# Gated cross-attention and expert layer on one core: the attention's output projection as three fp32r products of high and low parts, and the second norm applied by ScalarE

## The chip, the core and the metric

One core of a Trainium2 chip runs the whole program. The metric is the device time of one execution in microseconds (us), median of several runs. The granted TensorE clock over the profiled execution was 0.991 of full speed. The engines are named as in the profile: PE is TensorE (PEld its weight loads), DVE is VectorE, ACT is ScalarE, POOL is GpSimd, SP is SyncE, which here only starts transfers.

## The reference

```python
def xattn(query, key_value, Wq, bq, Wk, bk, Wv, bv, Wo, bo):   # 16 heads of 16
    q = (query @ Wq + bq).reshape(B, Nq, H, D).transpose(0, 2, 1, 3)
    k = (key_value @ Wk + bk).reshape(B, Nkv, H, D).transpose(0, 2, 1, 3)
    v = (key_value @ Wv + bv).reshape(B, Nkv, H, D).transpose(0, 2, 1, 3)
    attn = softmax(clip(einsum('bhqd,bhkd->bhqk', q, k) * D ** -0.5, -1e4, 1e4))
    x = einsum('bhqk,bhkd->bqhd', attn, v).reshape(B, Nq, Cq)
    return x @ Wo + bo
x = x + tanh(g_xattn[0]) * xattn(layernorm(x), ctx_768, ...)      # x: (8, 512, 256), ctx_768: (8, 512, 192)
x = x + tanh(g_ffn[0]) * ffn(layernorm(x), ...)                   # 8 experts of 1024, dense, gated by their logits
```

Everything is float32. The layer norm has no weights: `(x - mean) / sqrt(var + 1e-5)` over the 256 columns.

## The kernel before, in words

The program has three stages. The first (`build_project`, up to about 92 us) computes queries, keys and values of the 8 batch entries, as products of fp32r high and low parts, and stores them to DRAM. The second (`attend_programs`, about 92 to 537 us) is the attention, its output projection, the residual, the second layer norm and the expert logits. The third computes the eight experts (`expert_programs`), and its first tiles begin among the last steps of the second.

The change lies in the second stage. It runs a pass for each batch entry b, and the order in a pass is written out by hand. A pass has 4 groups g of 4 heads, each group 4 blocks k (the four 128-row tiles of keys), each block 4 places. A slot is written (g, k, place), a block (g, k). In a slot PE does one `scores_T` product (`ps_t`, L862: transposed scores of one head, 49 rows by 512 columns) and one `scores` product for the group two ahead (`ps_s`, L851, 48 rows). The two lie in different row halves of the array and start together, and I call them a pair. ACT takes `ps_t` with an exponential (L1170, into `probs_T` or `w_raw`), DVE takes `ps_s` with a row minimum (`low`, L1007). Each side has three banks, so that the pair of a slot waits for the exponential and the minimum of three slots before. At place 3 PE also does `probs_v` of the block before (`ps_o`, L873, 8 records).

Between these stand units, each of which fills the one bank `ps_m`, which has to be emptied before the next unit. The table `SHARED` says behind which pair PE does a unit, `VECTOR_AT` and `SCALAR_AT` at which slots DVE and ACT do their part of it. The entries are (kind, 0 for this batch entry or -1 for the one before, number). The kinds are:

- `low` (L879): the minima of a group turned, taken by ACT (L1181) and sent by SP into `q_st`;
- `out` (L884): the heads of a group turned, after ACT has copied `ps_o` into `o_sb` (`copy`, L1175); DVE divides by the sums (`normalise`, L1025 to L1030) into `attn`;
- `rows` (L890): `attn` of the entry before turned in two halves, taken by ACT as `attn_T` (L1186);
- `y` (L898, `project_out`): `attn_T` times `Wo`, in two halves of two token tiles. A tile is 2 fp32 products of 128 by 128 by 256 columns. The first half is done in two pieces, at (0, 3, 2) and (1, 0, 0) (`HALVES`). DVE adds it to the residual (`add_residual`, L1040);
- `x2T` (L905): the residual turned, taken by ACT; `xnT` (L911): the normed rows turned, taken by ACT as `x_hi` (L1198) and by DVE as `x_lo` (`split`, L1091);
- `logits` (L919, 4 fp32r products of 512 columns) and, once in four entries, `pick` (L926).

Without a bank, DVE does `statistics` (L1048) and `norm` (L1082: subtract the mean, multiply by the reciprocal root), `check` (L1013, L1015), and POOL computes the reciprocal root between those two (L803 to L827). The units with -1 belong to the entry before, so pass 0 has none of them, and after pass 7 a closing sequence does those of the last entry among the first tiles of the experts.

```python
    for k in range(TT):
        ...
        for place in range(GROUP):
            scores_T(b, g, k, place, turn)
            if exists(ahead[0]):
                scores(*ahead, place, turn + ahead[0] - b)
            if place == V_PLACE and exists(back[0]):
                probs_v(*back)
            first_half(b, HALVES.get((g, k, place)))
            shared(b, SHARED.get((g, k, place)))
```

## Time and profile before

| | |
|---|---|
| median of 3 runs | 1896.85 us (1896.41 to 1897.63) |
| the profiled execution, its own time | 1896.23 us |
| its span, first to last instruction | 1894.4 us |
| PE, DVE, ACT, POOL busy over the span | 98%, 68%, 67%, 8% |
| starts of the eight passes (first `ps_t`) | 112.4, 161.3, 212.0, 262.7, 313.4, 365.1, 415.8, 466.5 us |

The profile has one execution. Busy time of PE is that of its matmul records, whose ends are modelled, so a full PE row doesn't say that nothing waits: starts of neighbouring records say more. [...]

### The profile page before, as it was taken

The numbers are of one execution on the slowest core, as the hardware profiler recorded it, in microseconds if no ns is written. First come the engines' busy times: TensorE is split into PE (matmuls) and PEld (weight loads), VectorE is DVE, ScalarE is ACT, GpSimd is POOL, SyncE is SP. The second block draws the span as 40 slices with busy tenths as digits, with TensorE's granted clock in tenths as the row PEclk, the third lists the DMA queues.
The fourth block names the chain that finished last, engine by engine and source line by source line (L and its number), as shares of the span: only waits on it lengthen the run. The fifth ranks groups of instructions, "written<-read, shape, count | busy, mean of one in ns | idle before, by whom it ended". The sixth has DMA issues, their size and how long they took to land.

```text
span 1894.4 us, 25738 instructions
## 1 busy us (share of the span) xinstructions
PE 1862.6 (98%) x8868; PEld 1349.0 (71%) x8868; DVE 1291.1 (68%) x2279; ACT 1277.7 (67%) x2145; POOL 146.9 (8%) x327
## 2 busy tenths in 40 slices
...
GB/s 284 374 81 84 87 91 88 79 88 110 38 50 129 107 210 151 119 117 110 90 111 89 133 138 124 95 112 112 89 112 129 151 93 117 111 90 89 121 101 58
DMA packets 97245, 220.84 MB, mean 117 GB/s; under 512 B 31314, under 2 KB 49492, under 8 KB 87892
## 3 DMA queue, kind: packets, MB, share of 16 engines
...
q14 instruction: 64, 0.52, 0.1%
...
## 4 chain that ended last, share of the span: by engine, by line
PE 89%; ACT 3%; DVE 2%; issue 1%; POOL 0%; ACTq 0%; DVEq 0%; POOLq 0%
PE ps_y L2169 32%; PE ps_h L2116 28%; PE ps_t L862 7%; PE ps_o L873 6%; PE ps_h L2089 5%; PE ps_y L2101 4%; PE ps_s L851 2%; PE ps_m L898 2%; PE ps_m L884 1%; ACT w_raw L1170 1%; DVE low L1007 1%; PE ps_m L890 0%; ACT gelu L2366 0%; PE ps_m L919 0%; PE ps_m L905 0%
## 5 line engine op out<-in xcount | busy, mean ns | idle before, releaser
L2469 DVE TENSOR_TENSOR h_lo<-gelu,h_hi 128x512 fp32r<-128x512 f32 x512 | 352.8, 693 | 437.0 <-ACT h_hi L2369 405.7
L2116 PE MATMUL ps_h<-x_hi,w_pair 128*128 128x512 f32 x1568 | 562.3, 392 | 1.8 <-ACT gelu L2366 0.8
L2366 ACT ACTIVATE gelu<-early,b 128x512 f32<-128x512 f32 x336 | 243.2, 724 | 229.5 <-DVE early L2618 220.7
L2116 PEld LDWEIGHTS ps_h<-x_hi,w_pair 128*128 128x128 f32 x1568 | 294.3, 188 | 78.3 <-issue 6.0
L1007 DVE TENSOR_REDUCE low<-ps_s 128x1 f32<-128x512 f32 x512 | 322.1, 681 | 26.1 <-PE ps_s L851 23.1
L2369 ACT ACTIVATE h_hi<-gelu 128x512 fp32r<-128x512 f32 x448 | 283.5, 633 | 41.9 <-ACT gelu L2366 1.1
L2116 PE MATMUL ps_h<-x_lo,w_pair 128*128 128x512 f32 x784 | 309.4, 395 | 0.0
L2618 DVE TENSOR_TENSOR early<-ps_h,copy 128x512 f32<-128x512 f32 x336 | 230.5, 686 | 49.4 <-PE ps_h L2116 49.4
L1170 ACT ACTIVATE probs_T<-ps_t 128x512 f32<-128x512 f32 x384 | 206.4, 594 | 45.5 <-PE ps_t L862 44.6
L851 PE MATMUL ps_s<-k_st,q_st 48*128 48x512 f32 x512 | 205.0, 481 | 3.2 <-SPq L755 2.0
L2169 PE MATMUL ps_y<-h_hi,w_lo 128*128 128x512 f32 x512 | 202.7, 396 | 0.0
L2169 PE MATMUL ps_y<-h_hi,w_hi 128*128 128x512 f32 x512 | 202.4, 395 | 0.0
L2169 PE MATMUL ps_y<-h_lo,w_hi 128*128 128x512 f32 x512 | 202.0, 394 | 0.0
L862 PE MATMUL ps_t<-q_st,k_st 49*128 49x512 f32 x512 | 190.4, 456 | 3.6 <-ACT probs_T L1170 2.7
L862 PEld LDWEIGHTS ps_t<-q_st,k_st 49*128 49x128 f32 x512 | 84.0, 188 | 131.8 <-ACT probs_T L1170 54.3
L2116 PEld LDWEIGHTS ps_h<-x_lo,w_pair 128*128 128x128 f32 x784 | 147.2, 188 | 32.7
L2169 PE MATMUL ps_y<-h_hi,w_first_lo 128*128 128x512 f32 x384 | 152.0, 396 | 0.0
L2169 PE MATMUL ps_y<-h_hi,w_first_hi 128*128 128x512 f32 x384 | 151.8, 395 | 0.0
L2169 PE MATMUL ps_y<-h_lo,w_first_hi 128*128 128x512 f32 x384 | 151.6, 395 | 0.0
L2169 PEld LDWEIGHTS ps_y<-h_hi,w_lo 128*128 128x128 f32 x512 | 96.2, 188 | 23.2
L2169 PEld LDWEIGHTS ps_y<-h_hi,w_hi 128*128 128x128 f32 x512 | 96.0, 188 | 22.8
L2169 PEld LDWEIGHTS ps_y<-h_lo,w_hi 128*128 128x128 f32 x512 | 96.1, 188 | 22.3
...
## 6 DMA issues: line engine op xcount, KB each, us to landing
...
x_lo<-blocks_scratch SPq DMA_DIRECT2D x28, 768.0 KB, 10.2
...
q_st<-q_scratch SPq DMA_DIRECT2D x192, 64.0 KB, 2.3
k_st<-k_scratch SPq DMA_DIRECT2D x192, 64.0 KB, 2.3
...
```

Of the source, the lines that this page charges most:

```text
L851: pe.matmul(ps_s[bank_of(turn, at)][:], q_st[g][rows, j // 2, t * P:(t + 1) * P], k_st[g][rows, j // 2, :], start=True, stop=True).then_in ...
L862: pe.matmul(ps_t[bank_of(turn, at)][:], k_st[g][rows, j // 2, k * P:(k + 1) * P], q_st[g][rows, j // 2, :], start=True, stop=True).then_in ...
L873: mm = pe.matmul(ps_o[32 * j:32 * j + VW, :], v_st[g][:, k, j, :], probs_T[k][:, j, :], start=(k == 0), stop=(k == TT - 1))
L1007: dve.tensor_reduce(low[:, g % 2, column:column + 1], ps_s[bank_of(turn, at)][:], AX_X, ALU.min).then_inc(low_done, 1)
L1170: act.activation(probs_T[k][:, turned_head(b, g, k, i), :], ps_t[bank_of(turn, (g * TT + k) * GROUP + i)][:], ACT.Exp, scale=-1.0).then_in ...
L2089: mm = pe.matmul(ps_h[:, j % RING, :], w[:, k, at], x[:, k, bass.ds(c * SEQ, SEQ)], start=(i == 0), stop=(i == len(parts) - 1))
L2116: mm = pe.matmul(bank, w[wp], x[xp], start=start and n == 0, stop=n == 2, skip_group_check=not start)
L2169: mm = pe.matmul(ps_y[s][:, d, :], w[:, j, at], h[:, c, :], start=(i == 0 and c < 2 and m == 0), stop=(i == QUADS - 1 and c >= 2 and m == 2))
L2366: act.activation(gelu[:, c % GELUS, :], src, ACT.Gelu_apprx_tanh, bias=b1[p][:, j:j + 1]).then_inc(gelu_done, 1)
L2369: act.activation(h_hi[:, c, :], gelu[:, c % GELUS, :], ACT.Copy).then_inc(h_hi_done, 1)
L2469: dve.tensor_tensor(h_lo[:, j % RING, :], gelu[:, j % GELUS, :], h_hi[:, j % RING, :].bitcast(F32), ALU.subtract).then_inc(h_ready, 1)
L2618: dve.tensor_tensor(corner[c // 2], bank, copies[0 if c == 3 else 1][:], ALU.add).then_inc(corner_done, 1)
```

## The change

- `Wo` is loaded in the second stage (into the space of `attn`) and no longer in the first. ACT copies it to `wo_hi` and POOL subtracts it to `wo_lo`, both fp32r, once, before the first pass. PE and DVE wait for that.
- ACT's part of `rows` now writes `attn_hi` (fp32r), and DVE has a part of its own, `rows_low`, which writes `attn_lo` and frees the bank. `attn_lo` lies in the space of `xn`, so it also waits until `xn` of the entry before is turned.
- `project_out` does 6 fp32r products of 256 columns for a tile where there were 2 fp32 products: high by high, high by low, low by high, for both halves of the contraction.
- `norm` moves from DVE to ACT as `Identity` with scale (reciprocal root) and bias. POOL computes that bias, minus mean times root, with one more instruction. In the closing sequence DVE still does it.
- All three tables are written anew, `HALVES` excepted.
- `logits_T` holds one set of four entries and no longer two.

Per pass, the units of PE that stand at another slot are `out` of the entry before (0,1,2) to (0,1,1); `rows` 0 (0,2,2) to (0,1,2) and `rows` 1 (0,2,3) to (0,2,1); `low` 2 (1,1,3) to (1,0,3); `y` 1 (1,1,1) to (1,1,2); `out` 0 (1,2,0) to (1,2,2); `x2T` (1,3,0) and (2,0,2) to (1,3,1) and (2,0,1); `low` 3 (2,1,0) to (2,1,2); `out` 1 (2,2,1) to (2,2,0); `xnT` (2,3,1) and (3,0,0) to (2,3,2) and (3,0,2); `low` 0 of the next entry (3,1,3) to (3,1,0); `out` 2 (3,2,1) to (3,1,2); `logits` (3,3,0) to (3,2,1); `pick` (3,3,3) to (3,3,0).

```diff
 SHARED = {
-    (0, 0, 2): ("low", 0, 1), (0, 1, 2): ("out", -1, 3), (0, 2, 2): ("rows", -1, 0), (0, 2, 3): ("rows", -1, 1),
+    (0, 0, 2): ("low", 0, 1), (0, 1, 1): ("out", -1, 3), (0, 1, 2): ("rows", -1, 0), (0, 2, 1): ("rows", -1, 1),
...
 VECTOR_AT = {
+    (0, 1, 0): [("check", 0, 1), ("out", -1, 3)], (0, 1, 3): [("rows", -1, 0)], (0, 2, 3): [("rows", -1, 1)],
...
 SCALAR_AT = {
+    (0, 0, 1): [("low", 0, 1)], (0, 0, 2): [("copy", -1, 3)], (0, 1, 1): [("rows", -1, 0)], (0, 2, 2): [("rows", -1, 1)],
...
+    (2, 0, 3): [("copy", 0, 1)], (2, 1, 2): [("low", 0, 3), ("norm", -1, 0)], (2, 1, 3): [("norm", -1, 1)],
+    (2, 2, 0): [("norm", -1, 2)], (2, 2, 3): [("norm", -1, 3)], (2, 3, 1): [("xnT", -1, 0)], (3, 0, 1): [("xnT", -1, 1)],
...
@@ sync
+        sp.dma_start(wo_raw, io["Wo"].rearrange("(k p) n -> p k n", p=P)).then_inc(wo_loaded, 16)
@@ gpsimd
+        pool.wait_ge(wo_hi_done, 1)
+        pool.tensor_tensor(wo_lo[:], wo_raw, wo_hi[:].bitcast(F32), ALU.subtract).then_inc(wo_split, 1)
...
-            pool.tensor_tensor(rstd, root, dev, ALU.add).then_inc(rstd_done, 1)
+            pool.tensor_tensor(rstd, root, dev, ALU.add).then_inc(moment_done, 1)
+            pool.wait_ge(moment_done, first + 10)
+            pool.tensor_tensor(shift, mean, rstd, ALU.mult).then_inc(rstd_done, 1)
@@ tensor
+            parts = [(a, w, k) for k in range(KT) for a, w in ((attn_hi, wo_hi), (attn_hi, wo_lo), (attn_lo, wo_hi))]
             for t in tiles:
                 t0 = (2 * i + t) * P
-                for k in range(KT):
-                    mm = pe.matmul(ps_m[:, t * DIM:(t + 1) * DIM], attn_T[:, k, t0:t0 + P], wo[:, k, :],
-                                   start=(k == 0), stop=(k == KT - 1))
+                for n, (a, w, k) in enumerate(parts):
+                    mm = pe.matmul(ps_m[:, t * DIM:(t + 1) * DIM], a[:, k, t0:t0 + P], w[:, k, :],
+                                   start=(n == 0), stop=(n == len(parts) - 1))
@@ vector
+        def rows_low(b, i):
+            if i == 0:
+                wait(dve, in_psum["xnT"], b * KT)
+            dve.wait_ge(rows_hi_done, b * KT + i + 1)
+            dve.tensor_tensor(attn_lo[:, i, :], bank("rows", b, i)[:], attn_hi[:, i, :].bitcast(F32), ALU.subtract).then_inc(taken["rows"], 1)
@@ scalar
-            act.activation(attn_T[:, i, :], bank("rows", b, i)[:], ACT.Copy).then_inc(taken["rows"], 1)
+            act.activation(attn_hi[:, i, :], bank("rows", b, i)[:], ACT.Copy).then_inc(rows_hi_done, 1)
...
+        def layer_norm(b, t):
+            if t == 0:
+                act.wait_ge(rstd_done, b + 1)
+                wait(act, in_psum["xnT"], b * KT)
+            ins = act.activation(xn[:, t, :], x_res[:, t, :], ACT.Identity, bias=moments[:, 10, t:t + 1], scale=moments[:, 9, t:t + 1])
```

The order on PE in blocks (0,1) and (0,2) of pass 1, before, from the last pair ahead of `rows` 0 (the names of the rows are those of the units above; L862, L851, L873 and L890 are `scores_T`, `scores`, `probs_v` and `rows`):

```order
L862 MATMUL ps_t<-q_st,k_st 128x512 [waits b_exp_done]
L851 MATMUL ps_s<-k_st,q_st 128x512 [waits b_low_done]
L890 MATMUL ps_m<-ident,attn 128x128 [waits b_out_taken]
L890 MATMUL ps_m<-ident,attn 128x128 x3
L862 MATMUL ps_t<-q_st,k_st 128x512 [waits b_exp_done]
L851 MATMUL ps_s<-k_st,q_st 128x512 [waits b_low_done]
L873 MATMUL ps_o<-probs_T,v_st 17x512 [waits b_exp_done]
L873 MATMUL ps_o<-probs_T,v_st 17x512 x3
L890 MATMUL ps_m<-ident,attn 128x128 [waits b_out_taken,b_rows_taken]
L890 MATMUL ps_m<-ident,attn 128x128 x3
```

The same place of the change, from `out` of the entry before (L893) on; L871, L860, L882 and L899 are `scores_T`, `scores`, `probs_v` and `rows`:

```order
L893 MATMUL ps_m<-ident,o_sb 128x128 [waits b_o_copied,b_low_taken]
L893 MATMUL ps_m<-ident,o_sb 128x128 x3
L871 MATMUL ps_t<-q_st,k_st 128x512 [waits b_exp_done]
L860 MATMUL ps_s<-k_st,q_st 128x512 [waits b_low_done]
L899 MATMUL ps_m<-ident,attn 128x128 [waits b_out_taken]
L899 MATMUL ps_m<-ident,attn 128x128 x3
L871 MATMUL ps_t<-q_st,k_st 128x512 [waits b_exp_done]
L860 MATMUL ps_s<-k_st,q_st 128x512 [waits b_low_done]
L882 MATMUL ps_o<-w_raw,v_st 17x512 [waits b_exp_done,b_o_copied,b_v_loaded0]
L882 MATMUL ps_o<-w_raw,v_st 17x512 x3
```

`rows` 0, which waits for DVE's division, moved from a full block behind `out` to one pair behind it, and `rows` 1 no longer follows `probs_v` directly but stands behind the second pair of the next block.

The order on DVE in the same blocks of the change (L1036 to L1041 is the division, L1018 the minima, L1050 `rows_low`):

```order
L1036 RECIPROCAL recip<-ps_m 128x16 [waits b_out_taken,b_out_in_psum]
L1038 SCALAR_TENSOR_TENSOR fits<-ps_m,fits 128x16
L1041 TENSOR_TENSOR attn<-ps_m,recip 128x4x64 [waits b_recip_done]
L1018 TENSOR_REDUCE low<-ps_s 128x1 [waits b_scores_in_psum] x3
L1050 TENSOR_TENSOR attn_lo<-ps_m,attn_hi 128x512 [waits b_rows_hi_done]
L1018 TENSOR_REDUCE low<-ps_s 128x1 [waits b_scores_in_psum] x4
L1050 TENSOR_TENSOR attn_lo<-ps_m,attn_hi 128x512 [waits b_rows_hi_done]
```

The division stands behind one minimum of block (0,1) where it stood behind four, and the two new subtractions follow three and four minima later.

## Rows read from the trace of the kernel before

**Rows 1.** The page: busy time of each engine, share of the span, instructions.

```profile
PE 1862.6 (98%) x8868; PEld 1349.0 (71%) x8868; DVE 1291.1 (68%) x2279; ACT 1277.7 (67%) x2145; POOL 146.9 (8%) x327
```

**Rows 2.** Busy time of PE, PEld, DVE, ACT, POOL in pass 3.

```profile
262.68:313.40 50.72, 50.47 (x324) 22.36 (x320) 47.55 (x97) 39.69 (x80) 5.33 (x16) 1.00 0.32 85
```

**Rows 3.** Timeline of PE, pass 3, (0,1) to (0,2): start us, us, what.

```profile
265.50 0.50 PE L862 MATMUL ps_t<-q_st,k_st 49*128 49x512 f32 x1
...
265.84 0.39 PE L862 MATMUL ps_t<-q_st,k_st 49*128 49x512 f32 x1
...
266.09 0.40 PE L862 MATMUL ps_t<-q_st,k_st 49*128 49x512 f32 x1
266.44 0.66 PE L884 MATMUL ps_m<-ident,o_sb 128*128 128x128 f32 x4
267.02 0.49 PE L862 MATMUL ps_t<-q_st,k_st 49*128 49x512 f32 x1
...
267.45 1.05 PE L873 MATMUL ps_o<-w_raw,v_st 128*17 128x512 f32 x8
268.44 0.50 PE L862 MATMUL ps_t<-q_st,k_st 49*128 49x512 f32 x1
```

**Rows 4.** The same view: two of the three `y` pieces.

```profile
272.83 1.13 PE L898 MATMUL ps_m<-wo,attn_T 128*128 128x256 f32 x4
273.89 0.50 PE L862 MATMUL ps_t<-q_st,k_st 49*128 49x512 f32 x1
...
279.42 1.99 PE L898 MATMUL ps_m<-wo,attn_T 128*128 128x256 f32 x8
281.34 0.49 PE L862 MATMUL ps_t<-q_st,k_st 49*128 49x512 f32 x1
```

**Rows 5.** The same view in the first stage: products of 256 columns.

```profile
41.69 0.28 PE L275 MATMUL ps_v<-wv_lo,ctx_hi 128*128 128x256 f32 x1
...
42.16 0.28 PE L275 MATMUL ps_v<-wv_hi,ctx_lo 128*128 128x256 f32 x1
```

**Rows 6.** Groups by line: weight loads of those products, up to 960 us.

```profile
L275 PEld LDWEIGHTS ps_v<-wv_hi,ctx_hi 128*128 128x128 f32 x64 | 12.1, 189 | 0.0
```

**Rows 7.** Timeline of PE, pass 3, blocks (2,3) and (3,1).

```profile
299.53 0.39 PE L862 MATMUL ps_t<-q_st,k_st 49*128 49x512 f32 x1
299.69 0.50 PE L851 MATMUL ps_s<-k_st,q_st 48*128 48x512 f32 x1
300.12 1.05 PE L873 MATMUL ps_o<-probs_T,v_st 128*17 128x512 f32 x8
...
304.09 0.50 PE L862 MATMUL ps_t<-q_st,k_st 49*128 49x512 f32 x1
...
305.36 0.50 PE L862 MATMUL ps_t<-q_st,k_st 49*128 49x512 f32 x1 [0.25 <-ACT probs_T L1170]
...
305.83 1.05 PE L873 MATMUL ps_o<-w_raw,v_st 128*17 128x512 f32 x8
```

**Rows 8.** Timeline of ACT, pass 3: `copy` of the entry before.

```profile
265.64 0.60 ACT L1175 ACTIVATE o_sb<-ps_o 128x512 f32<-128x512 f32 x1 [0.30 <-PE ps_o L873]
```

**Rows 9.** Timeline of DVE, pass 3: the division for one group.

```profile
296.82 0.25 DVE L1025 RECIPROCAL recip<-ps_m 128x16 f32<-128x16 f32 x1
...
297.10 0.42 DVE L1030 TENSOR_TENSOR attn<-ps_m,recip 128x256 f32<-128x256 f32 x1
```

**Rows 10.** Groups by line, up to 960 us: minima, norm and `x_lo`.

```profile
L1007 DVE TENSOR_REDUCE low<-ps_s 128x1 f32<-128x512 f32 x512 | 322.1, 681 | 26.1 <-PE ps_s L851 23.1
L1082 DVE TENSOR_SCALAR xn_b<-x_res,moments_b 128x256 f32<-128x256 f32 x32 | 12.6, 404 | 0.0
L1091 DVE TENSOR_TENSOR x_lo<-ps_m,x_hi 128x512 fp32r<-128x512 f32 x15 | 10.2, 680 | 2.7 <-ACT x_hi L1198 2.7
```

**Rows 11.** Timeline of POOL, pass 3: first and last instruction of the root.

```profile
284.15 0.20 POOL L803 TENSOR_TENSOR moments_b<-stats_b 128x4 f32<-128x4 f32 x1 [19.79 <-DVE stats_b L1048]
...
288.44 0.20 POOL L827 TENSOR_TENSOR moments_b<-moments_b 128x4 f32<-128x4 f32 x1
```

More of the change, by code:

```diff
@@ L540 @@
 SHARED = {
-    (0, 0, 2): ("low", 0, 1), (0, 1, 2): ("out", -1, 3), (0, 2, 2): ("rows", -1, 0), (0, 2, 3): ("rows", -1, 1),
-    (1, 0, 0): ("y", -1, 0), (1, 1, 1): ("y", -1, 1), (1, 1, 3): ("low", 0, 2), (1, 2, 0): ("out", 0, 0),
-    (1, 3, 0): ("x2T", -1, 0), (2, 0, 2): ("x2T", -1, 1), (2, 1, 0): ("low", 0, 3), (2, 2, 1): ("out", 0, 1),
-    (2, 3, 1): ("xnT", -1, 0), (3, 0, 0): ("xnT", -1, 1), (3, 1, 3): ("low", 1, 0), (3, 2, 1): ("out", 0, 2),
-    (3, 3, 0): ("logits", -1, 0), (3, 3, 3): ("pick", -1, 0),
+    (0, 0, 2): ("low", 0, 1), (0, 1, 1): ("out", -1, 3), (0, 1, 2): ("rows", -1, 0), (0, 2, 1): ("rows", -1, 1),
+    (1, 0, 0): ("y", -1, 0), (1, 0, 3): ("low", 0, 2), (1, 1, 2): ("y", -1, 1), (1, 2, 2): ("out", 0, 0),
+    (1, 3, 1): ("x2T", -1, 0), (2, 0, 1): ("x2T", -1, 1), (2, 1, 2): ("low", 0, 3), (2, 2, 0): ("out", 0, 1),
+    (2, 3, 2): ("xnT", -1, 0), (3, 0, 2): ("xnT", -1, 1), (3, 1, 0): ("low", 1, 0), (3, 1, 2): ("out", 0, 2),
+    (3, 2, 1): ("logits", -1, 0), (3, 3, 0): ("pick", -1, 0),
 }
@@ L795, in gpsimd @@
         more_consts(pool)
+        pool.wait_ge(wo_hi_done, 1)
+        pool.tensor_tensor(wo_lo[:], wo_raw, wo_hi[:].bitcast(F32), ALU.subtract).then_inc(wo_split, 1)
         def reciprocal_root(b):
-            mean, dev, diff, square, spread, var, root, root_2, scaled, rstd = (moments[:, i, :] for i in range(10))
-            first = b * 9
+            mean, dev, diff, square, spread, var, root, root_2, scaled, rstd, shift = (moments[:, i, :] for i in range(11))
+            first = b * 10
             pool.wait_ge(stats_done, b * 2 + 2)
@@ L975, in tensor @@
         pe.wait_ge(consts_set, 11)
+        pe.wait_ge(wo_split, 1)
         for b in range(BATCH):
@@ L1107, in set_flag @@
         def set_flag():
+            for i in range(KT):
+                rows_low(LAST, i)
             dve.wait_ge(fits_in_psum, 1)
             dve.tensor_scalar(keep["clip_flag"][:], ps_t[BANKS - 1][:, 0:1], 3 * HEADS * TOKENS - 0.5, None, ALU.is_lt).then_inc(fits_summed, 1)
-        take = {"out": normalise, "y": add_residual, "xnT": split, "pick": keep_logits,
-                "check": check_lows, "statistics": statistics, "norm": layer_norm}
+        take = {"out": normalise, "rows": rows_low, "y": add_residual, "xnT": split, "pick": keep_logits,
+                "check": check_lows, "statistics": statistics}
         def batch(b, turn):
```

59 lines of the change are left out of this document (33 added, 26 removed).

## The prediction

> **What bounds the kernel now.** I read the page first: PE is busy for 98% of the span, DVE and ACT for two thirds [rows 1]. Then the sums of one pass of the second stage, where the change lies: of 50.72 us PE is busy for 50.47, DVE for 47.55, ACT for 39.69 [rows 2]. So PE sets the pace, DVE has only 3 us in hand, ACT has 11. The third view is the timeline of PE, for what a unit really costs: the starts of neighbouring rows tell it. In block (0,1) of pass 3 a pair comes 0.34 us after the first of the block, the next 0.25 later, the unit `out` 0.35 after that; `out` takes 0.58; the pair behind it needs 0.43 before `probs_v` may start, and `probs_v` 0.99 until the next pair [rows 3]. A block without a unit would thus take about 0.34 + 0.24 + 0.24 + 0.33 + 0.98 = 2.13 us. A unit inside the run of pairs costs its own time and a **break** of 0.2 (0.35 ahead of it for 0.24, and 0.43 behind for 0.33); right behind `probs_v` it costs no break, since the run is over there anyway. The fourth thing to see is where PE waits. In block (3,1) the first `ps_t` starts at 304.09 and the fourth only at 305.36, 1.27 later where 0.82 would do, because the bank comes back from the exponential of three slots before, and `probs_v` follows 0.47 later for 0.33: 0.60 us lost, as that block had no unit inside [rows 7]. In (2,3) the fourth `ps_t` (299.53) was on time, but its `ps_s` came at 299.69, when DVE had freed the bank, and `probs_v` at 300.12: 0.59 for 0.33, so 0.26 lost [rows 7].
>
> **The products of the projection.** Two pieces of 4 records take 1.06 us to the next pair, the third of 8 records 1.92 [rows 4]: 4 records are 0.86 (0.215 each), and 0.20 lies around them. Per pass that is 1.06 + 1.06 + 1.92 = 4.04. In place of 4 records stand 6 fp32r products of 256 columns. Such products, each with its own weights, start 0.47 / 4 = 0.1175 us apart in the first stage [rows 5]. So 6 take 0.71 + 0.20 = 0.91 and 12 take 1.41 + 0.20 = 1.61; per pass 3.43, a gain of **0.61**. The recorded weight load of these products is 0.189 us long [rows 6], longer than the 0.1175 between starts, so the loads do run beside the products of the same rows of the array. The Trainium skill (TensorE: Matmul & The Clock Gate, "What overlaps and what doesn't") says that a weight load overlaps running products only when they use other rows of the array; by that rule the 24 loads that stand here for 16 would lie open, and it speaks against this change. The trace doesn't agree; what it would cost is among the rivals.
>
> **The places on PE.** Before, three units of a usual pass stood behind `probs_v` (`rows` 1, `low` 2, `low` 0 of the next entry); now only `low` 2 does. Two more breaks: **+0.40**.
>
> In block (0,1), times from its first pair (265.50), `out` now stands behind the second pair and wants to start at 0.34 + 0.33 = 0.67. `copy` starts at +0.14, set by PE's own `ps_o` [rows 8], and ends at +0.74; with 0.05 of handing over (my estimate for a semaphore) `out` starts at 0.79, 0.12 late. The next pair is then at 1.37 and `rows` 0 wants to start at 1.80. But it needs the division: the records of `out` end 0.66 after their start [rows 3], at 1.45; the division takes 0.70 (296.82 to 297.52) [rows 9]; with two hand-overs that is 2.25, so `rows` 0 waits 0.45. Together **+0.57**. Queued behind it are the next pair and `probs_v`. Behind ACT's copy of `rows` 0 stand two exponentials, needed only a block later.
>
> In block (3,1) `low` 0 and `out` 2 now fill the time in which PE waited: **-0.60**. But `logits` leaves (3,3), and in five of the passes (1, 2, 3, 5, 6) that block has no unit at all: the same wait there, **+0.60**. In pass 4 `pick` fills it, with a break of 0.2.
>
> **DVE.** It gives up the norm (four times 0.404) and gets two subtractions like `x_lo` (0.680) [rows 10]: nearly even, so DVE stays at about 47.4. What moves is where it is late. The norms stood at (1,3), (2,0), (2,1) and (2,2), so the wait in (2,3) and one in (1,3), that I take as large, go: **-0.52**. In exchange the division of `out` 1 moves ahead of three minima of block (2,2). From its first pair: the first minimum can start at about 0.66 (0.50 of its product and a hand-over), 0.60 for it, 0.63 for the division, which overlaps its neighbours a little, three minima of 0.60 to 0.63 (322.1 us for 512) [rows 10], so the last ends at about 3.77. The third pair of (2,3) is due at 2.90 + 0.58 = 3.48 and needs that bank: 0.34 late, and 0.1 more, as rows 7 show 0.26 lost for 0.16 late: **+0.44**. In (1,1) `y` now stands behind the third pair, whose bank DVE frees late after the first residual: +0.1, of 0 to 0.3.
>
> **ACT and POOL.** No row shows the norm on ACT. By rows it lies between the DVE instruction of the same size, 0.40, and an ACT copy of 512 columns, 0.60 [rows 8, 10]; I take 0.45, as it has half the columns, so 1.8 us per pass. ACT's 11 us of idle time hide it. It can start when POOL is done: the root took 4.49 us [rows 11], one instruction more makes it 4.8, and from `statistics` 3 at (1,3,2), about 26.7 us into the pass by such counting of blocks, that is 31.5; ACT comes to slot (2,1,2) at 31.6. The exponential behind it is needed 2 us later, so about a microsecond of lateness costs nothing, and beyond it each tenth costs a tenth. The load of `Wo`, ACT's copy and POOL's subtraction have the 20 us from the start of the stage to the first pass (112.4): nothing, unless the load lands very late, and then once.
>
> **The sum.** A usual pass: -0.61 + 0.40 + 0.57 - 0.60 + 0.60 - 0.52 + 0.44 + 0.1 = **+0.38**, five times: +1.9. Pass 4: without the empty block and with `pick`'s break, 0.38 - 0.60 + 0.20 = 0.0. Pass 7 has no minima from its middle on, so waits for DVE in (2,3) neither go nor come, and (3,1) and (3,3) cancel: -0.61 + 0.40 + 0.57 - 0.26 + 0.1 = +0.2. Pass 0 has no units of an entry before: 0, of -0.3 to +0.3. The closing sequence has 16 records of `y` (-0.62), but PE waits for two DVE subtractions one after the other where it had to wait for ACT alone: about +0.35, so -0.27. In all 1.9 + 0.0 + 0.2 + 0 - 0.27 = **+1.8 us**. Against the profiled execution (1896.23) that gives 1898.0; its time is 0.6 below the median, so I say **1898.5** for the median.
>
> **The rivals.**
> 1. *The new waits don't come.* The hand-over in (0,1) is quicker, and DVE, without the norm, is ahead in (2,3) and (1,1). For it: DVE has time in hand in each pass. Against: the chain in (0,1) is made of durations that rows 8 and 9 show. Without 0.57, 0.44 and 0.1 a usual pass is at -0.73, five of them -3.7, pass 4 at -1.1, pass 7 at -0.5, closing -0.27: -5.6, or **1891.3**. With half of them, 1894.9.
> 2. *The first piece of `y` waits for `attn_lo` (slower).* `rows` 1 has now two takers in series, ACT at (0,2,2) and DVE at (0,2,3), each behind its own queue. By the same count `attn_lo` is ready about 0.9 into block (0,3), where `y` wants it: there is no margin. For it: one more exponential ahead (0.5) or one more minimum (0.6) puts PE that much behind, in seven passes. With 0.6 each, +4.2, **1902.7**; with both, 1906. It decides from 0.3 us per pass on. Against: DVE is not behind at this place in the pass before.
> 3. *Weight loads lie open*, as by the rule above: 24 times 0.189 is 4.5 us per pass and 36 in all [rows 6], **1934**. The rows of the first stage speak against it.
> 4. *The products aren't single records*: fp32r tiles that run as two would take 24 times 0.43 us per pass. Rows 5 show one record each; I give it 1 in 100.
>
> **How the numbers follow.** About 0.2% (3.8 us) is what a measurement of this kernel can tell from no change. My forecast, a few small terms that nearly cancel, has 0.52. Rival 1 has 0.20 and lies on the faster side, rival 2 has 0.25 and lies on the slower side in its full size, rivals 3 and 4 have 0.02 and 0.01. Faster 0.20, same 0.52, slower 0.28. The range goes from 1892.5, most of rival 1, to 1903.0, rival 2 with one instruction late.
>
> **What would show it right or wrong.** In the profile after, 6 products of `y` should lie 0.12 apart and a piece of 12 take 1.6 us. `rows` 0 in (0,1) should start about 1.5 us after `out`, and block (0,1) last 4.2 us for 2.94 (265.50 to 268.44). Block (3,3) should last 2.7 and (3,1) 3.3. A pass should take 51.0 to 51.1 us. If block (0,1) is shorter than 3.9, rival 1 holds; if block (0,3) is over 3.6 us, rival 2. The forecast is wrong if a pass lies outside 50.3 to 51.5.

## The result, and the profile after

The changed kernel takes **1916.4 us** (median of 8 runs, 1906.6 to 1924.3) where the kernel before takes 1896.6 beside it (1894.9 to 1898.1): a ratio of 1.0101, with a 95% interval of 1.0084 to 1.0117. It is slower by about 20 us; the forecast was 1898.5, within 1892.5 to 1903.0. Its profiled execution took 1914.5 us, with a span of 1912.7. The line of the page that answers to [rows 1]:

```profile
PE 1870.1 (98%) x8932; PEld 1347.8 (70%) x8932; DVE 1303.2 (68%) x2267; ACT 1292.4 (68%) x2174; POOL 149.5 (8%) x335
```

The shares tell nothing. The sums by pass do: busy time of PE, PEld, DVE, ACT, POOL, then the granted clock, DMA share and GB/s. Passes 1, 3, 4, 6 and 7 of the changed kernel (pass 3 answers to [rows 2]):

```profile
159.73:216.17 56.44, 54.75 (x334) 23.02 (x330) 49.87 (x95) 41.44 (x83) 6.62 (x18) 0.91 0.29 77
...
268.37:319.23 50.86, 50.08 (x333) 21.82 (x330) 47.95 (x92) 41.43 (x83) 7.15 (x18) 1.00 0.32 85
319.23:373.42 54.19, 52.78 (x340) 23.19 (x336) 49.76 (x101) 41.44 (x83) 7.02 (x18) 0.97 0.29 80
...
424.72:479.00 54.28, 52.24 (x332) 22.32 (x328) 49.94 (x94) 41.58 (x83) 7.16 (x18) 0.97 0.34 99
479.00:530.89 51.89, 48.65 (x290) 20.16 (x286) 33.93 (x67) 39.81 (x80) 6.81 (x18) 0.97 0.18 50
```

Pass 3 takes 50.86 us, 0.14 more than before, where 0.38 was forecast. But pass 1 takes 5.8 us more than pass 1 before (50.69), pass 4 2.5 and pass 6 3.6, and in all three the granted clock is below 1, which it never was before in passes 1 to 7. Passes that do the same work and differ by 5 us are the first thing to explain. The extra lies in the first two blocks: (0,0) and (0,1) take 5.99 and 6.74 us in pass 1, 2.83 and 4.37 in pass 3. The timelines of DVE, then POOL, then PE around the start of pass 1 (start us, us, what; in brackets the idle time before it and who ended it):

```profile
157.57 1.29 DVE L1018 TENSOR_REDUCE low<-ps_s 128x1 f32<-128x512 f32 x2 [0.24 <-PE ps_s L860]
158.77 2.09 DVE L1024 SCALAR_TENSOR_TENSOR fits<-low,fits 128x16 f32<-128x16 f32 x1
160.78 0.16 DVE L1026 SCALAR_TENSOR_TENSOR fits<-low,fits 128x16 f32<-128x16 f32 x1
```

```profile
158.44 2.38 POOL L840 TENSOR_TENSOR x_res<-x_res,bo_gated 128x1024 f32<-128x1024 f32 x1 [56.61 <-DMA x_res<-in_x]
```

```profile
160.07 0.39 PE L871 MATMUL ps_t<-q_st,k_st 49*128 49x512 f32 x1
161.60 0.50 PE L860 MATMUL ps_s<-k_st,q_st 48*128 48x512 f32 x1 [1.15 <-DVE low L1018]
...
163.15 0.79 PE L871 MATMUL ps_t<-q_st,k_st 49*128 49x512 f32 x1
```

`check`, two instructions on 16 columns of 0.16 us each, takes 2.09 us in its first half (the row of 2.09 against the next one of 0.16). That half ends at 160.86, 0.04 behind POOL's bias addition to `x_res` (158.44 to 160.82), which adds the output bias to the input rows of an entry and which I call the addition from here on. DVE comes late to the minima, PE has no free bank of `ps_s` and idles 1.15 us, and from 162.3 on PE runs at the lower of its two levels: a `ps_t` record takes 0.79 us for 0.50. The sums of the stretch behind it show a clock of 0.50, which is 1.2 GHz for 2.4:

```profile
162.84:172.50 9.66, 9.48 (x38) 3.23 (x37) 5.84 (x13) 4.38 (x9) 0.00 (x0) 0.50 0.19 51
```

The same meeting stands ahead of six of the seven passes, and the one without it is the shortest. Undisturbed, passes 1 to 6 take 50.9 us, but 51.5 for pass 4, which has `pick`, and pass 7 takes 49.9 (the first experiment below). Start of the addition, start of `check`, time that the slowed half of `check` took, and the length of the pass behind it:

| addition starts | `check` starts | slowed half | pass behind |
|---|---|---|---|
| 158.44 | 158.77 | 2.09 us | 56.4 |
| 214.52 | 215.22 | 1.72 | 52.2 |
| 267.67 | 267.42 | none (`check` ended as the addition started) | 50.9 |
| 317.62 | 318.27 | 1.77 | 54.2 |
| 370.87 | 372.72 | 0.57 | 51.3 |
| 423.80 | 423.77 | 2.37 (its second half) | 54.3 |
| 477.15 | 478.05 | 1.54 | 51.9 |

Before, `check` and the addition never met. Here are SP's issue of the load of `x_res`, `check`, and the addition: first of the kernel before in passes 3 and 5, then of the changed one, where only the issue stands:

```profile
308.82 0.40 SPq L752 DMA_DIRECT2D x_res<-in_x  x1
...
413.70 0.16 DVE L1013 SCALAR_TENSOR_TENSOR fits<-low,fits 128x16 f32<-128x16 f32 x1
...
415.22 2.39 POOL L831 TENSOR_TENSOR x_res<-x_res,bo_gated 128x1024 f32<-128x1024 f32 x1 [24.16 <-DMA x_res<-in_x]
```

```profile
313.52 0.40 SPq L756 DMA_DIRECT2D x_res<-in_x  x1
```

Two things moved towards each other. `check` went from (3,3,0) to (3,3,1). And the load is issued 45.15 us into pass 3 for 46.14, since SP issues it behind the sending of `low` 0 of the next entry, and that unit went from (3,1,3) to (3,1,0). The addition follows the issue by 3.7 to 4.1 us in both kernels, with one exception: the load of the first row above, whose addition started 6.6 us later, at 315.45. Before, `check` ended 1.3 us ahead of the addition in pass 5 and 1.0 to 1.3 in five others; what the addition met then, up to the last pass, were instructions that read PSUM (minima, and in one pass `pick`).

The other forecasts can be read in the undisturbed pass 3. A piece of `y`, first product and the pair behind it, and `out` with `rows` 0 in block (0,1):

```profile
279.41 0.38 PE L908 MATMUL ps_m<-wo_hi,attn_hi 128*128 128x256 f32 x1
279.63 0.28 PE L908 MATMUL ps_m<-wo_lo,attn_hi 128*128 128x256 f32 x1
279.75 0.28 PE L908 MATMUL ps_m<-wo_hi,attn_lo 128*128 128x256 f32 x1
...
280.31 0.50 PE L871 MATMUL ps_t<-q_st,k_st 49*128 49x512 f32 x1
```

```profile
272.07 0.63 PE L893 MATMUL ps_m<-ident,o_sb 128*128 128x128 f32 x4
...
273.60 0.63 PE L899 MATMUL ps_m<-ident,attn 128*128 128x128 f32 x4 [0.47 <-DVE attn L1041]
```

The products lie 0.12 apart, the piece takes 0.90 (0.91 forecast) and the piece of 12 takes 1.61 (1.61 forecast); `rows` 0 starts 1.53 behind `out` (1.5) after a wait of 0.47 (0.45).

### The profile page after: what moved, and what is told of

Read it like the earlier page. It is cut to its first block, busy times and chain, and to the rows that moved or that the text cites. A ratio compares the mean times of both kernels' runs of the same rounds, so it can differ in the third digit from the quotient of the medians.

```text
span 1912.7 us, 25907 instructions
## 1 busy us (share of the span) xinstructions
PE 1870.1 (98%) x8932; PEld 1347.8 (70%) x8932; DVE 1303.2 (68%) x2267; ACT 1292.4 (68%) x2174; POOL 149.5 (8%) x335
## 4 chain that ended last, share of the span: by engine, by line
PE 78%; DVE 2%; ACT 2%; issue 1%; POOL 0%; DVEq 0%; ACTq 0%
PE ps_y L2201 32%; PE ps_h L2148 28%; PE ps_h L2121 4%; PE ps_y L2133 4%; PE ps_t L871 3%; PE ps_o L882 3%; PE ps_m L908 1%; PE ps_s L860 1%; ACT w_raw L1190 1%; PE ps_m L893 0%; ACT gelu L2398 0%; PE ps_m L899 0%; DVE out_T_acc L2592 0%; PE ps_m L929 0%; ACT probs_T L1190 0%
## 5 line engine op out<-in xcount | busy, mean ns | idle before, releaser
L1018 DVE TENSOR_REDUCE low<-ps_s 128x1 f32<-128x512 f32 x512 | 321.5, 681 | 26.9 <-PE ps_s L860 24.6
L860 PE MATMUL ps_s<-k_st,q_st 48*128 48x512 f32 x512 | 210.4, 486 | 7.8 <-DVE low L1018 5.8
L871 PE MATMUL ps_t<-q_st,k_st 49*128 49x512 f32 x512 | 198.0, 465 | 3.9 <-ACT probs_T L1190 2.2
L871 PEld LDWEIGHTS ps_t<-q_st,k_st 49*128 49x128 f32 x512 | 84.5, 190 | 146.9 <-ACT probs_T L1190 75.2
## 6 DMA issues: line engine op xcount, KB each, us to landing
x_lo<-blocks_scratch SPq DMA_DIRECT2D x28, 768.0 KB, 10.2
```

Source lines behind the costliest of these rows:

```text
L860: pe.matmul(ps_s[bank_of(turn, at)][:], q_st[g][rows, j // 2, t * P:(t + 1) * P], k_st[g][rows, j // 2, :], start=True, stop=True).then_in ...
L871: pe.matmul(ps_t[bank_of(turn, at)][:], k_st[g][rows, j // 2, k * P:(k + 1) * P], q_st[g][rows, j // 2, :], start=True, stop=True).then_in ...
L1018: dve.tensor_reduce(low[:, g % 2, column:column + 1], ps_s[bank_of(turn, at)][:], AX_X, ALU.min).then_inc(low_done, 1)
```

## The experiments

### `check` moved out of the way

```diff
-    (3, 0, 2): [("xnT", -1, 1)], (3, 1, 2): [("out", 0, 2)], (3, 3, 0): [("pick", -1, 0)], (3, 3, 1): [("check", 1, 0)],
+    (3, 0, 2): [("xnT", -1, 1)], (3, 1, 2): [("out", 0, 2)], (3, 2, 1): [("check", 1, 0)], (3, 3, 0): [("pick", -1, 0)],
```

> The changed kernel with one thing moved: DVE's `check` of the next entry goes from slot (3,3,1) to (3,2,1), some 2 us ahead of POOL's bias addition. Theory A (in the changed kernel this `check`, an instruction with two operands in SBUF, meets POOL's 2.4 us addition and is held until it ends; PE starves behind it and its clock falls): every `check` takes 0.16 us, passes 1 to 6 last 50.8 to 51.2 us each (for 56.4, 52.2, 50.9, 54.2, 51.3, 54.3), no stretch of lowered clock between 130 and 500 us, time 1898 to 1902. Theory B (the places of ACT and PE in blocks (0,0) and (0,1) are to blame, the `check` only waits along): passes stay uneven, blocks (0,0) and (0,1) together stay above 9 us in passes 1, 4 and 6, time above 1908.

Measured: **1897.87 us** beside 1897.59 for the kernel before, ratio 1.0006 (0.9997 to 1.0015). One entry of a table gives back the whole loss. The durations of `check` in ns (minimum, median, maximum), first in the changed kernel and then here, and passes 1 and 3 here:

```profile
L1024 DVE SCALAR_TENSOR_TENSOR fits<-low,fits x32: 159/167/2086, 102.9 to 514.2; 128x16 f32<-128x16 f32 x32
```

```profile
L1024 DVE SCALAR_TENSOR_TENSOR fits<-low,fits x32: 161/164/176, 102.6 to 502.4; 128x16 f32<-128x16 f32 x32
```

```profile
162.20:213.07 50.87, 49.82 (x332) 21.72 (x329) 47.93 (x95) 41.32 (x83) 6.66 (x18) 1.00 0.32 85
...
263.97:314.87 50.90, 50.07 (x334) 21.68 (x330) 47.92 (x95) 41.42 (x83) 7.10 (x18) 1.00 0.32 85
```

Passes 1 to 6 last 50.87, 50.90, 50.90, 51.49, 50.87 and 50.96 us, all at full clock. Theory B of the expectation falls.

### The addition moved instead, `check` left at (3,3,1)

```diff
+        def load_x_res(b):
+            wait(sp, in_psum["x2T"], b * KT)
+            wait(sp, xn_ready, b * 2)
+            sp.dma_start(x_res[:], io["x"][bass.ds(b * SEQ, SEQ), :].rearrange("(t p) d -> p t d", p=P)).then_inc(x_loaded, 16)
...
                 ahead = group_after(b, g, 3)
+                if g == GROUPS - 1 and exists(b):
+                    load_x_res(b)
...
-            if exists(b):
-                wait(sp, in_psum["x2T"], b * KT)
-                wait(sp, xn_ready, b * 2)
-                sp.dma_start(x_res[:], io["x"][bass.ds(b * SEQ, SEQ), :].rearrange("(t p) d -> p t d", p=P)).then_inc(x_loaded, 16)
```

> The changed kernel with its tables untouched, `check` at (3,3,1): only SP issues the load of x_res earlier, ahead of the loads that follow the third group (some 38 us into a pass for 45), so that POOL's bias addition runs about 42 to 44 us into a pass, 5 us ahead of `check`. Theory A (the coincidence of the two is the cause): every `check` takes 0.16 us, passes 1 to 6 last 50.9 us, time 1896 to 1900. Theory B (the slot (3,3,1) itself delays DVE or PE, whatever POOL does): passes uneven as in the change, 1907 or more.

Measured: **1901.57 us** beside 1896.14, ratio 1.0027 (1.0018 to 1.0036). Passes 1 to 6 are as with `check` moved (50.87 the first, row below), so the slot (3,3,1) is harmless when POOL is idle. The 4 us by which it is slower than with `check` moved lie in pass 0, which has no norm to wait for: there the load comes earlier still, and the addition meets the `check` at (2,3,3). Blocks (3,0) to (3,2) of that pass take 5.0 us more than in the change. DVE, POOL, then the sums of passes 0 and 1:

```profile
147.92 1.16 DVE L1027 SCALAR_TENSOR_TENSOR fits<-low,fits 128x16 f32<-128x16 f32 x1
```

```profile
146.67 2.37 POOL L843 TENSOR_TENSOR x_res<-x_res,bo_gated 128x1024 f32<-128x1024 f32 x1 [45.21 <-DMA x_res<-in_x]
```

```profile
112.17:164.23 52.06, 49.76 (x266) 19.36 (x264) 44.01 (x83) 35.59 (x71) 2.37 (x1) 0.82 0.25 68
164.23:215.10 50.87, 49.87 (x332) 21.85 (x328) 47.93 (x95) 41.30 (x83) 6.27 (x17) 1.00 0.31 85
```

I had not foreseen this. It is the same mechanism at another place: `check` ends 0.04 behind the addition again, and PE's clock is at half for 10 us from 151.1 on.

### The collision put into the kernel before

```diff
-    (3, 3, 0): [("check", 1, 0)], (3, 3, 3): [("pick", -1, 0)],
+    (3, 3, 3): [("check", 1, 0), ("pick", -1, 0)],
```

> The kernel before with one thing moved: `check` of the next entry goes from slot (3,3,0) to (3,3,3), where POOL's bias addition is under way in six of seven entries (it runs from about 0.7 us before a pass begins to 1.8 after). Theory A: there `check` takes 1.3 to 2.3 us in place of 0.16, blocks (0,0) and (0,1) grow by 1 to 3 us, the clock falls behind some of them; 6 times 1 to 3 us gives 1903 to 1915. Theory B (places of the change to blame): nothing else is changed here, so 1896 to 1898.

Measured: **1912.17 us** (1907.80 to 1924.64) beside 1897.59, ratio 1.0086 (1.0061 to 1.0111). Without a line of the change, one moved entry makes nearly its whole loss. DVE, POOL, and the sums of passes 1 and 3:

```profile
161.55 1.83 DVE L1013 SCALAR_TENSOR_TENSOR fits<-low,fits 128x16 f32<-128x16 f32 x1
163.30 0.16 DVE L1015 SCALAR_TENSOR_TENSOR fits<-low,fits 128x16 f32<-128x16 f32 x1
```

```profile
160.97 2.38 POOL L831 TENSOR_TENSOR x_res<-x_res,bo_gated 128x1024 f32<-128x1024 f32 x1 [60.98 <-DMA x_res<-in_x]
```

```profile
161.31:216.54 55.23, 53.68 (x325) 23.44 (x321) 49.22 (x97) 39.51 (x79) 6.17 (x17) 0.94 0.29 78
...
271.66:323.40 51.74, 50.80 (x324) 22.41 (x320) 48.43 (x97) 39.67 (x80) 5.20 (x16) 1.00 0.32 84
```

Pass 3 shows what the wait alone costs: 51.74 for 50.72, 1.0 us. In pass 1 PE waits 1.25 us where it waits 0.71 in pass 3, and has the clock at half for 6.8 us behind it: 4.5 us. In passes 1 to 7 of this profile the clock is at half for 20.4 us, which is up to 10.2 us of the 15.9 that they are longer. **The larger part of the loss is the clock**, not the wait.

### What is it that meets

The changed kernel, with a `check` that has one operand; the tile that it no longer adds to starts at the full count instead.

```diff
-            dve.scalar_tensor_tensor(out=fits[:, 0, :], in0=low[:, g % 2, :], scalar=FITS, in1=fits[:, 0, :],
-                                     op0=ALU.is_le, op1=ALU.add)
...
+            dve.tensor_scalar(spare[:, 0, :], low[:, g % 2, :], FITS, None, ALU.is_le)
+            dve.tensor_scalar(spare[:, 1, :], low[:, g % 2, :], -FITS, None, ALU.is_ge).then_inc(lows_checked, 1)
```

> The changed kernel, `check` at (3,3,1) as in it, but of one SBUF operand: it compares `low` with its bound by tensor_scalar and writes the flags to a tile of their own. Left out: the flags are not added up, the count starts at its full value instead. If it is the second SBUF operand that makes the instruction wait for POOL: both take about 0.16 us although the addition is under way, passes 50.9 us, time 1897 to 1900. If any DVE instruction between SBUF tiles is held: 0.6 to 2.4 us as in the change, 1907 to 1920.

Measured: **1918.19 us** beside 1897.96, ratio 1.0107 (1.0093 to 1.0122). With one operand in SBUF and no other input tile it is held just the same; DVE, then POOL:

```profile
162.90 1.97 DVE L1026 TENSOR_SCALAR spare<-low 128x16 f32<-128x16 f32 x1
```

```profile
162.46 2.37 POOL L842 TENSOR_TENSOR x_res<-x_res,bo_gated 128x1024 f32<-128x1024 f32 x1 [60.95 <-DMA x_res<-in_x]
```

So the second operand isn't what decides here. In all these traces POOL's addition held `fits<-low,fits`, `spare<-low`, the cast `w_first_hi<-early` (2.04 us for 0.68 with `check` moved) and `w_first_lo<-early,w_first_hi` (3.30 for 1.23, in the kernel before). It held none of the instructions that read PSUM: minima at 0.68, `x_lo<-ps_m,x_hi` at 0.69, the division at 0.42. One of them is nearly a twin of `check`, of the same operation and size, with one input in PSUM. It ran in 0.11 us in the middle of an addition (the kernel with the addition moved, DVE and POOL):

```profile
412.38 0.11 DVE L1041 SCALAR_TENSOR_TENSOR fits<-ps_m,fits 128x16 f32<-128x16 f32 x1
```

```profile
411.59 2.38 POOL L843 TENSOR_TENSOR x_res<-x_res,bo_gated 128x1024 f32<-128x1024 f32 x1 [11.73 <-DMA x_res<-in_x]
```

The hold also goes the other way. In the last pass of the kernel before, a cast was under way (504.75 to 505.43) when the addition came, and the addition took 2.72 us where it takes 2.37 to 2.42 with nothing of that kind ahead of it; then it held `w_first_lo` in turn (POOL, DVE):

```profile
504.96 2.72 POOL L831 TENSOR_TENSOR x_res<-x_res,bo_gated 128x1024 f32<-128x1024 f32 x1 [12.55 <-DMA x_res<-in_x]
```

```profile
505.47 3.30 DVE L1863 TENSOR_TENSOR w_first_lo<-early,w_first_hi 128x1024 fp32r<-128x1024 f32 x1
```

The Trainium skill (SBUF — State Buffer, "Who interferes with whom") says that DVE and GpSimd share a pair of ports as an exclusive lock, taken by a DVE instruction with two SBUF inputs against a GpSimd instruction that reads SBUF, and by copy, cast and tensor_scalar when they run in a mode with two ports; the second to come waits for the whole first. The traces agree: two SBUF inputs were held, and so were the tensor_scalar and the cast. Which mode these two ran in no trace shows. `check` ends 0.04 us behind the addition, the cast 0.55 and `w_first_lo` 1.09, each its own usual time less 0.12 to 0.14: they stood still until POOL had ended and then ran at full speed.

### The products alone, and with the norm

The changed kernel with `SHARED`, `SCALAR_AT` and `VECTOR_AT` of the kernel before and this entry for `attn_lo`, the norm being on DVE again; the second kernel has the norm on ACT, at the slots of the change. The lines with - are those of the kernel before, then of the first kernel.

```diff
-    (0, 1, 3): [("out", -1, 3)], (0, 2, 1): [("check", 0, 1)], (1, 0, 0): [("y", -1, 0)],
+    (0, 1, 3): [("out", -1, 3)], (0, 2, 1): [("check", 0, 1)], (0, 2, 3): [("rows", -1, 0)], (0, 3, 0): [("rows", -1, 1)], (1, 0, 0): [("y", -1, 0)],
```

> The changed kernel with all units at the slots of the kernel before: of the change only the three fp32r products stay (ACT writes attn_hi and DVE attn_lo, at (0,2,3) and (0,3,0)); the norm is on DVE again, as rstd times x plus a shift, and `check` is at (3,3,0). By the prediction's terms: 7 times -0.61 and -0.27 in the closing, against DVE's two subtractions more (1.36 us per pass), which may cost up to 0.3 per pass: 1892 to 1895. By the rival of open weight loads: 4.5 us per pass more, 1930 or so.

```diff
-    (2, 0, 3): [("x2T", -1, 1), ("copy", 0, 1)], (2, 1, 0): [("low", 0, 3)], (2, 3, 1): [("xnT", -1, 0)],
+    (2, 0, 3): [("x2T", -1, 1), ("copy", 0, 1)], (2, 1, 0): [("low", 0, 3)], (2, 1, 2): [("norm", -1, 0)], (2, 1, 3): [("norm", -1, 1)],
+    (2, 2, 0): [("norm", -1, 2)], (2, 2, 3): [("norm", -1, 3)], (2, 3, 1): [("xnT", -1, 0)],
```

> As the kernel with the products alone, and the norm on ACT at the slots that the change gives it, (2,1,2) to (2,2,3). By the prediction's terms DVE's waits in the second half of a pass go, -0.52 in each of five to seven passes, and ACT's time costs nothing: 1889 to 1893. If ACT's four instructions (0.58 us each) hold up exponentials instead, 1893 to 1898.

Measured: **1917.81 us**, ratio 1.0111 (1.0093 to 1.0129), and **1920.09**, ratio 1.0116 (1.0101 to 1.0132), beside 1897.59. Both far outside what I expected, and neither has a collision with `check`. What PE waited for in pass 2 of the products alone, in us:

```profile
PE ps_m L908 <- DVE attn_lo L1050: 1.0, 1, 1.0
PE ps_m L899 <- DVE attn_lo L1050: 1.0, 1, 1.0
```

All units share one bank, and with `attn_lo` ACT and DVE take it one after the other. At the slots of the kernel before, `rows` 1 stands one pair behind `rows` 0, and `y` three behind that: each waits 1.0 us. A pass is 52.4 us for 50.7, and here too the clock falls in four passes. This is the mechanism of rival 2, in the slots in which it comes true; in the slots of the change, block (0,3) takes 3.26 us (rival 2 asked for over 3.6) and PE waits for neither. So the products lose at the old places, and at the new ones these two waits are gone. Between the two kernels, in passes with an undisturbed clock, the norm on ACT makes a pass 0.3 us longer (52.69 for 52.38), where I had -0.52: blocks (2,2), (2,3) and (3,0) take 0.09, 0.14 and 0.07 more, and (1,3) takes 3.01 in both.

### The products against plain fp32 ones, in the same slots

```diff
-            parts = [(a, w, k) for k in range(KT) for a, w in ((attn_hi, wo_hi), (attn_hi, wo_lo), (attn_lo, wo_hi))]
+            parts = [(attn_hi, wo_hi, k) for k in range(KT)]
...
-                    mm = pe.matmul(ps_m[:, t * DIM:(t + 1) * DIM], a[:, k, t0:t0 + P], w[:, k, :],
+                    mm = pe.matmul(ps_m[:, t * DIM:(t + 1) * DIM], a[:, k, t0:t0 + P].bitcast(F32), w[:, k, :].bitcast(F32),
```

> The changed kernel with `check` at (3,2,1), and the projection as plain fp32 products again, one per 128 rows of attn_hi and wo_hi, in the same slots; ACT and DVE still write both parts. Left out: the products with the low parts. It differs from the kernel with `check` at (3,2,1) by the products alone. By the prediction's first term (0.91 for 1.06, 1.61 for 1.92): blocks (0,3), (1,0), (1,1) longer by 0.15, 0.15 and 0.31, 0.61 per pass, seven times 4.3, and up to 0.6 in the closing: 1902 to 1903 for 1897.9. If part of a piece's time is filled by waits for ps_t and ps_s banks anyway, 0.2 to 0.4 per pass: 1899 to 1901.

A plain fp32 product is two records in these traces and an fp32r product one. Measured: **1902.70 us** beside 1896.29, ratio 1.0039 (1.0025 to 1.0053), against 1.0006 with the three products. Blocks (0,3), (1,0) and (1,1) take 3.42, 3.58 and 4.46 us for 3.25, 3.42 and 4.16, so 0.63 per pass where 0.61 was forecast. The first term of the sum is right, and the fp32r products are worth 5 to 6 us here (4.9 by passes 1 to 7 and the closing of the two profiles, 6 by the ratios).

### Two smaller losses, and a version that beats both kernels

On top of `check` at (3,2,1): `rows` 0 moved behind `probs_v`, with its takers; `first_weights`, in which DVE splits the first expert's weights into `w_first_hi` and `w_first_lo`, moved one block later in the last pass; both.

```diff
-    (0, 0, 2): ("low", 0, 1), (0, 1, 1): ("out", -1, 3), (0, 1, 2): ("rows", -1, 0), (0, 2, 1): ("rows", -1, 1),
+    (0, 0, 2): ("low", 0, 1), (0, 1, 1): ("out", -1, 3), (0, 1, 3): ("rows", -1, 0), (0, 2, 1): ("rows", -1, 1),
```

> The changed kernel with `check` at (3,2,1), and `rows` 0 behind `probs_v`, at (0,1,3) in place of (0,1,2) (its takers ACT at (0,1,3), DVE at (0,2,0)). If the wait of `rows` 0 for the division is what makes block (0,1) last 4.37 us, as the prediction's term of 0.45 says, that wait goes and with it one break of 0.2: block (0,1) 3.7 to 3.8, seven times -0.6, time 1893.5 to 1895. If something else fills the block, the time stays within 1 us of 1897.9.

```diff
-                    if (b, g, k) == (LAST, GROUPS - 1, 0):
+                    if (b, g, k) == (LAST, GROUPS - 1, 1):
```

> The changed kernel with `check` at (3,2,1), and in the last pass DVE's first_weights behind (3,1) in place of (3,0), so behind POOL's last bias addition (508.55 to 510.94) and behind the division of `out` 2. Theory A: the cast w_first_hi no longer takes 2.04 us for 0.68, PE's wait of 1.15 us for the division before `logits` goes: block (3,2) of the last pass 3.0 for 4.18, time 1 to 1.5 us below 1897.9. Rival: PE then waits for the weights at the start of the next stage: no change or up to 2 us slower.

> All three moves on top of the change: `check` at (3,2,1), `rows` 0 behind `probs_v`, first_weights behind (3,1). If the terms add: 1897.9 - 4.2 - 1.2 = 1892.5, so 1891.5 to 1894, 0.2% below the kernel before. If they hide each other, 1894 to 1897.

Measured: `rows` 0 later **1907.78 us** (1901.75 to 1913.44) beside 1897.96, ratio 1.0059 (1.0045 to 1.0074); first_weights later 1898.40, ratio 1.0005 (0.9996 to 1.0014); both 1905.59, ratio 1.0041 (1.0028 to 1.0054).

All three missed the gain that I expected. `rows` 0 later did what was expected in its own block, 3.77 for 4.37, and then PE stood before `rows` 1 for 1.2 us in each pass, since the one bank came back later (pass 3):

```profile
PE ps_m L899 <- DVE attn_lo L1050: 1.2, 1, 1.2
```

The wait changed places and grew. In the profiled execution, the fastest of the six, the clock fell behind none of these waits and its mean is 0.992; the other five have 0.984 to 0.990, so it seems to have fallen in them, but they have no profile. With first_weights later, block (3,2) of the last pass takes 2.97 us for 4.18, as expected, but from the last `ps_t` to the end it then takes 1380.8 us for 1380.3, and the medians can't tell the rest from nothing.

The lesson of `rows` 0 gave the next edit: a whole block between units that ACT and DVE both take. Their takers move with them, as far behind as before.

```diff
-    (0, 0, 2): ("low", 0, 1), (0, 1, 1): ("out", -1, 3), (0, 1, 2): ("rows", -1, 0), (0, 2, 1): ("rows", -1, 1),
-    (1, 0, 0): ("y", -1, 0), (1, 0, 3): ("low", 0, 2), (1, 1, 2): ("y", -1, 1), (1, 2, 2): ("out", 0, 0),
+    (0, 0, 2): ("low", 0, 1), (0, 1, 1): ("out", -1, 3), (0, 2, 1): ("rows", -1, 0), (0, 3, 1): ("rows", -1, 1),
+    (1, 0, 2): ("y", -1, 0), (1, 0, 3): ("low", 0, 2), (1, 1, 2): ("y", -1, 1), (1, 2, 2): ("out", 0, 0),
...
-HALVES = {(0, 3, 2): ("y", -1, 0)}
+HALVES = {}
```

> The changed kernel with `check` at (3,2,1), and the units from `rows` 0 to `y` 0 spread: `rows` 0 at (0,2,1), `rows` 1 at (0,3,1), the whole of `y` 0 (12 products, no half ahead) at (1,0,2), each with its takers as far behind as before. The units share one bank of ps_m, so each must be taken by ACT and then DVE before the next starts: with a block between them none should wait. Blocks (0,1), (0,2), (0,3) 2.9 each for 4.37, 2.90, 3.25, block (1,0) 4.1 for 3.42: -1.1 us per pass, passes of 49.8, seven times that is -7.7: time 1890 to 1892, 0.3% below the kernel before. If `y` 0 waits for attn_lo in (1,0) in place of it, 1895 to 1899.

> As the kernel with the spread units, and first_weights behind (3,1) in the last pass: block (3,2) of it 3.0 for 4.2, so up to 1.2 us below the one with the spread units alone, 1889 to 1892. If the stage behind takes the gain back, as the run with first_weights later alone suggests, no difference from it.

Measured: **1893.86 us**, ratio 0.9986 (0.9977 to 0.9995), and with first_weights later **1892.85**, ratio 0.9982 (0.9973 to 0.9991), both beside 1896.14. These beat the kernel before, by 3 us, and the change, by over 20; the two can't be told apart. PE waits at most 0.3 us at a time in passes 4 and 5 of the first. The sums of its pass 5, and of the last pass of the second:

```profile
361.97:412.18 50.21, 49.51 (x334) 21.77 (x330) 47.91 (x95) 41.54 (x84) 4.82 (x17) 1.00 0.32 86
```

```profile
462.86:510.83 47.97, 46.29 (x290) 19.68 (x286) 30.85 (x64) 39.56 (x80) 6.76 (x18) 1.00 0.21 57
```

A pass is 0.69 shorter than with `check` moved alone, not 1.1: block (0,1) takes 3.18 us and (0,3) 3.16, where I had 2.9 for each.

## Why the prediction was wrong

**The step that failed** is the one on DVE, "what moves is where it is late", together with "ACT and POOL". It counted what DVE's instructions cost by their usual rows, and never looked at what each shares with another engine. The move of `check` by one slot isn't named in the prediction at all, and POOL's addition isn't either (of POOL it names the root and the subtraction of `Wo`): both stand at nothing in the sum, and moving `check` out of their meeting gave back 18 of the 19 us, by the two ratios. Yet the trace of the kernel before had the signs: the addition of 2.4 us once per pass, and in the last pass `w_first_lo` at 3.3 us for 1.23 under it. A queue was left out too: the move of `low` 0, which I priced on PE alone (-0.60), lets SP issue the load of `x_res` 1 us sooner, and so shifts POOL's addition. None of the four rivals had a term for an instruction held by another engine, nor for the clock. The prediction's own last sign came true: four of the passes 1 to 6 lie outside 50.3 to 51.5 us.

**The size.** In the profiled executions, passes 1 to 7 take 371.2 us in the change and 355.9 with `check` moved: 15.3 us. The clock was at half for 10.2, 3.4, 3.4 and 6.8 us in them or right behind the last (from 162.3, 322.7, 428.6 and 527.5 on); 20.4 us of these lie in the passes, and half of that is 10.2 us lost if PE bounds throughout. That leaves 5.1 for the waits, and PE's idle times of over 0.6 us in these passes sum to 6.0, of which 1.2 are there with `check` moved too. The stretch of 6.8 us reaches beyond the passes, and from the last `ps_t` to the end the change takes 1.6 us more. Pass 0 goes the other way: in the profiled execution of the change it takes 47.15 us, with `check` moved 49.95, for the clock, at half from about 94 us on in every one of these kernels, came back up at 121.3 us in the one and at 128.7 in the other. So the two profiled executions differ by 14.4 us and the medians by 18.5. The spread of the runs is of that kind: the fastest, 1906.6, has a mean clock of 0.989, the slowest, 1924.3, of 0.979.

**What was right.** With the collision gone, the kernel is at 1897.87, and the forecast was 1898.5; as the points below show, that is closer than the terms deserve. Point by point, from pass 3 of that run:

- the products: -0.61 forecast, 0.63 measured. Weight loads lie beside the products as [rows 5, 6] said (0.187 us long, products 0.12 apart); rival 3 is out, and rival 4, one record each.
- block (0,1): 4.2 forecast, 4.37 measured, by the wait that was named. The hand-over of 0.05 was too small: `out` starts 0.145 us behind the end of `copy`, and `rows` 0 0.146 behind the end of the division, which makes up the difference. Rival 1 (under 3.9) is out.
- (3,1) 3.3 and (3,3) 2.7 forecast, 3.33 and 2.73 measured.
- (2,3): the term of +0.44 was wrong in its size. The block takes 3.15 us, as before (3.16), where 3.34 follows from the terms; neither the gain of 0.26 there nor the loss came. In (1,3) a block of 2.90 for 3.22 looks like the gain, but it isn't shown to come from the norm: with the products alone, the norm still on DVE, (1,3) takes 3.01, and moving the norm to ACT left it at 3.01. So no run shows the -0.52, and what the norm on ACT did by itself was +0.3.
- (1,1): 4.16 for 4.50, of which 0.31 is the products: nothing for a forecast of +0.1.
- A usual pass: 50.9 for a forecast of 51.0 to 51.1, which is +0.2 for +0.38.
- ACT's norm: 0.45 forecast, 0.58 measured, although it has half the columns of the copy that takes 0.60. It also reads a scale and a bias for each partition, which the copy doesn't; what each of the two is worth no run here separates:

```profile
L1224 ACT ACTIVATE xn_b<-x_res,moments_b 128x256 f32<-128x256 f32 x28 | 16.4, 584 | 0.0
```

- Pass 7: +0.2 forecast, +2.2 measured (49.87 for 47.69). 1.2 of it is POOL again: the cast `w_first_hi` held for 2.04 us, and this time with the division of `out` 2 and PE's `logits` behind it. Some 0.7 is ACT: blocks (2,2) and (2,3) take 2.97 and 3.06 us for 2.65 each, with the four norms in them; between the kernels with the products alone and with the norm the same two blocks go from 2.65 each to 3.01 and 3.08. "ACT's 11 us of idle time hide it" was wrong, in this pass most of all, where no minima slow PE.
- Closing: -0.27 forecast. From the last `ps_t` to the end it takes 1380.3 us, and took 1380.3 before: nothing.

The errors of the small terms nearly cancel, and that is luck: pass 7 alone missed by 2.0 us, the five usual passes by 0.8 the other way. The profiles give +3.0 us for passes 1 to 7 and the closing, against the forecast of +1.8.
